# A vision block with written-out engine programs: maxima rows zeroed by a transfer, second norm from accumulators and ScalarE squares, a 64-row low part on GpSimd

## The reference

```
h = patches(images, 16x16, with 4 shifted copies) @ W + b       # 196 tokens of 192 per image
h = [cls_tok, h]                                                # 197 tokens
h = h + attention(layernorm(h))     # 6 heads of 32, scale 32**-0.5, a key-independent bias from
                                    # q . anchor; softmax over 197 keys; output product with Wo
x = clip(round(layernorm(h) / 0.02), -128, 127) as int8
h = h + (x @ weight_int8) * 0.0002 + bias
```

## Time and profile before

| what | value |
|---|---|
| median of the runs shown | 1684.41 us |
| the profiled execution, its own time | 1684.14 us |
| its span in the trace | 1682.2 us |
| TensorE busy | 1603.4 us, 95% |
| VectorE busy | 1491.4 us, 89% |
| ScalarE busy | 870.8 us, 52% |
| GpSimd busy | 822.2 us, 49% |
| first stage | to about 415 us |
| attention stage, all engines at work | about 445 to 1655 us |

### The profile page before, as it was taken

The page is one execution under the profiler, slowest core; times in us unless marked ns, Lnnn a source line. Parts: engine busy times, 40 slices in busy tenths (PEclk is TensorE's granted clock), DMA queues, the critical chain, the costliest instruction groups (busy, mean ns, idle before and its releaser), DMA issues.

```text
span 1682.2 us, 53448 instructions
## 1 busy us (share of the span) xinstructions
PE 1603.4 (95%) x16880; PEld 1426.5 (85%) x16880; DVE 1491.4 (89%) x3656; ACT 870.8 (52%) x2014; POOL 822.2 (49%) x1787
## 2 busy tenths in 40 slices
PE   3999999998499999999999999999999999999995
PEld 3999999998488888888888888888888888888884
DVE  7888888887479999999999999999999999999995
ACT  2000000000367767677767676777767776777663
POOL 3353535355025555555554555555555555555555
PEclk9999999999599999999999999999999999999997
DMA  9998999993435444444444444444444444444431
GB/s 300 271 313 292 305 299 309 292 332 131 138 130 164 152 160 137 161 150 154 144 154 159 147 151 149 161 144 157 142 159 148 159 139 156 156 153 146 153 110 37
DMA packets 213037, 303.64 MB, mean 181 GB/s; under 512 B 44656, under 2 KB 201891, under 8 KB 202868
## 3 DMA queue, kind: packets, MB, share of 16 engines
q1 hardware_dynamic: 201618, 227.16, 41.7%
q10 hardware_dynamic: 7378, 39.47, 8.1%
q0 software_dynamic: 3984, 36.28, 5.6%
HBM read 126.54 MB, written 58.29 MB: 110 GB/s over the span
## 4 chain that ended last, share of the span: by engine, by line
PE 71%; DVE 1%; POOL 1%; issue 1%; ACT 1%; ACTq 0%; DMA 0%; SPq 0%; POOLq 0%; DVEq 0%
PE o_bank L945 12%; PE bank L937 11%; PE bank L891 11%; PE s_pair L925 9%; PE bank L912 7%; PE bank L900 7%; PE bank L872 5%; PE o_bank L975 5%; PE bank L1037 2%; PE bank L1075 1%; PE o_bank L967 0%; ACTq L769 0%; DVE neg_max L1195 0%; ACT probs L1091 0%; DMA xn_in<-xn_scratch 0%
## 5 line engine op out<-in xcount | busy, mean ns | idle before, releaser
L1091 ACT ACTIVATE probs<-bank 99x396 f32<-99x396 f32 x768 | 380.5, 495 | 163.1 <-PE bank L937 156.5
L356 PE MATMUL bank<-e_t,xt 128*128 128x192 f32 x2352 | 387.0, 328 | 26.6 <-DVE xt L464 21.8
L356 PEld LDWEIGHTS bank<-e_t,xt 128*128 128x128 f32 x2352 | 385.5, 191 | 27.8 <-DVE xt L464 27.6
L1195 DVE TENSOR_REDUCE neg_max<-s_pair 99x4 f32<-99x788 f32 x384 | 374.2, 974 | 16.7 <-PE s_pair L925 15.8
L1352 POOL TENSOR_TENSOR hb<-h,ffn_bias 99x384 f32<-99x384 f32 x128 | 129.6, 1012 | 381.6 <-DVE h L1285 381.6
L937 PE MATMUL bank<-st 128*99 128x198 f32 x1536 | 296.5, 274 | 5.0 <-ACT probs L1091 5.0
L937 PEld LDWEIGHTS bank<-st 128*99 128x99 f32 x1536 | 194.9, 165 | 87.2 <-issue 80.0
L464 DVE STREAM_TRANSPOSE xt<-x_t 128x256 f32<-128x256 f32 x588 | 214.9, 416 | 44.4 <-PE bank L356 42.4
L945 PE MATMUL o_bank<-probs,vals 99*32 99x198 f32 (+1 forms) x3072 | 223.5, 337 | 0.0
L925 PE MATMUL s_pair<-st 128*99 128x198 f32 x1536 | 217.9, 264 | 3.1 <-DVE neg_max L1195 2.2
L1340 POOL TENSOR_SCALAR qx<-h,ln 99x192 f32<-99x192 f32 x256 | 199.0, 782 | 41.3 <-POOL ln L163 41.3
(11 more groups left out here) (140 smaller groups left out, 3612.2 us busy)
## 6 DMA issues: line engine op xcount, KB each, us to landing
st<-qk_hi SPq DMA_DIRECT2D x378, 198.0 KB, 2.3
st<-qk_lo SPq DMA_DIRECT2D x189, 198.0 KB, 2.3
x_t<-in_x_dram SPq DMA_DIRECT2D x26, 1344.0 KB, 20.8
x_t<-in_x_dram ACTq DMA_DIRECT2D x26, 1344.0 KB, 23.1
xn_in<-xn_scratch SPq DMA_DIRECT2D x128, 148.5 KB
h_in<-h_scratch SPq DMA_DIRECT2D x128, 148.5 KB
h_scratch<-h_t POOLq DMA_DIRECT2D x13, 1344.0 KB, 18.2
xn_scratch<-xn_t POOLq DMA_DIRECT2D x13, 1344.0 KB, 8.9
```

The source lines that it names most:

```text
L356: last = pe.matmul(token_bank(p)[:, 0:D], xt[:, p, c // 3, c % 3, :], e_t[:, row_kind(t), col, c // 3, c % 3, :], start=c == 0, stop=c == 5)
L1091: nc.scalar.activation(probs[:, n.two, h, :, :], wide(T_BANK, TC), ACT.Exp).then_inc(exp_done, 1)
L1195: nc.vector.tensor_reduce(out=neg_max[:, n.two, :, 2 * j:2 * j + 2].rearrange("p c h -> p h c"), in_=both, axis=AX_X, op=ALU.max, negate=T ...
```

## The change

The rows of maxima are set to zero by one more transfer for a pair of images (`clear_maxima`, from a tile of zeros; 2 x 6 x 396 values), so `stacked[pair]` counts ten; for that the running `shift` goes, and VectorE splits `neg_max` itself. The residual h1 is made by two instructions of 192 columns instead of one of 384, each of which also gives the sum of its row (`h_sum`). BN_STATS and `pair_factors` go. GpSimd makes the negated mean from the sum (2 columns), ScalarE squares h1 minus the mean in two ACTIVATEs of 192 columns, whose bias is that mean (one value a row) and which also give the sums of their squares (`h_var`), and GpSimd makes the factor from these with two small instructions. The 64-row low part goes from VectorE to GpSimd, behind `a_lo`, with a wait between them.

```diff
+            def clear_maxima(p):
+                if p.reuses(MOD):
+                    sp.wait_ge(st_done, p.count(H, (2 - MOD) * H))
+                sp.dma_start(q_st[MAX_HI:MAX_LO + 1:4, p.pair, :, :, :].rearrange("p h s n -> p h (s n)").bitcast(F32),
+                             zero_rows[:].unsqueeze(1).broadcast_to([2, H, 2 * TP])).then_inc(stacked[p.pair], 16)
...
@@ SyncE, odd step
                     sp.wait_ge(qklo_done, p.pair_count(3, 2))
                     stack(p, 1, 1, qk_lo)
+                    clear_maxima(p)
...
@@ ScalarE, step: behind high(p, ...), ahead of exps(c, 4)
+                if has_q:
+                    act.wait_ge(mean_done, q.count(1, 1))
+                    for cc in range(2):
+                        nc.scalar.activation(square[:, cc, :], h1[:, q.two, cc, :], ACT.Square,
+                                             bias=ln2[:, q.two, 0, cc:cc + 1],
+                                             accum_out=h_var[:, q.two, cc:cc + 1]).then_inc(var_done, 1)
                 if has_c:
                     exps(c, 4)
...
@@ VectorE, step
-                if has_e:
-                    dve.wait_ge(ahi_done, e.count(1, 1))
-                    nc.vector.tensor_tensor(a_mix[DB:DA, e.two, 1, :], att_t[0:DB, 1, :],
-                                            a_mix[0:DB, e.two, 1, :].bitcast(F32), ALU.subtract).then_inc(alo_done, 1)
                 if has_a:
                     dve.wait_ge(max_done, a.count(HG, HG))
-                    nc.vector.tensor_tensor(shift[:, a.slot, :, :], shift[:, a.slot, :, :], neg_max[:, a.two, :, :],
-                                            ALU.add).then_inc(shift_done, 1)
-                    dve.wait_ge(shift_done, a.count(1, 1))
                     if a.reuses(NS):
                         dve.wait_ge(mt_done, a.count(1, 1 - NS))
-                    nc.vector.tensor_copy(max_parts[:, a.two, :, 0:H], shift[:, a.slot, :, :]).then_inc(mpart_done, 1)
+                    nc.vector.tensor_copy(max_parts[:, a.two, :, 0:H], neg_max[:, a.two, :, :]).then_inc(mpart_done, 1)
...
-                    nc.vector.tensor_tensor(h1[:, e.two, :, :], h_in[:, e.two, :, :], rows(MISC[0]),
-                                            ALU.subtract).then_inc(h1_done, 1)
+                    for cc in range(2):
+                        last = nc.vector.scalar_tensor_tensor(out=h1[:, e.two, cc, :], in0=h_in[:, e.two, cc, :], scalar=1.0,
+                                                              in1=rows(MISC[0])[:, cc, :], op0=ALU.mult,
+                                                              op1=ALU.subtract, accum_out=h_sum[:, e.two, cc:cc + 1])
+                    last.then_inc(h1_done, 1)
...
-                if has_e:
-                    dve.wait_ge(h1_done, e.count(1, 1))
-                    for cc in range(2):
-                        last = nc.vector.bn_stats(st2[:, e.two, cc, :], h1[:, e.two, cc, :])
-                    last.then_inc(st2_done, 1)
...
@@ GpSimd, step
-                    pool.wait_ge(st2_done, q.count(1, 1))
-                    pair_factors(nc, link, st2[:, q.two, :, :], v, ln2[:, q.two, :, :].rearrange("p j c -> p c j"),
-                                 minus_half[0:TC, 0:2])
+                    pool.wait_ge(var_done, q.count(2, 2))
+                    pool.sem_inc(passed, 1)
+                    link(nc.gpsimd.tensor_scalar(var, h_var[:, q.two, :], 4.0 / D, 4.0 * LN_EPS, ALU.mult, ALU.add))
+                    link(nc.gpsimd.tensor_tensor(factor, var, minus_half[0:TC, 0:2], ALU.pow))
...
                     nc.gpsimd.tensor_tensor(a_lo[:, e.two, :], att_t[:, 0, :], a_mix[:, e.two, 0, :].bitcast(F32),
                                             ALU.subtract).then_inc(pool_lo, 1)
+                    pool.wait_ge(pool_lo, e.count(1, 1))
+                    nc.gpsimd.tensor_tensor(a_mix[DB:DA, e.two, 1, :], att_t[0:DB, 1, :],
+                                            a_mix[0:DB, e.two, 1, :].bitcast(F32), ALU.subtract).then_inc(alo_done, 1)
+                    pool.wait_ge(alo_done, e.count(1, 1))
...
                     pool.wait_ge(h1_done, e.count(1, 1))
+                    nc.gpsimd.tensor_scalar(ln2[:, e.two, 0, :], h_sum[:, e.two, :], -1.0 / D, 0.0, ALU.mult,
+                                            ALU.add).then_inc(mean_done, 1)
```

More of the change, by code:

```diff
@@ L682, in build_attention @@
     query_row = tile("query_row", [DA, 1])
-    shift = tile("shift", [TC, MOD, 2, H])
+    zero_rows = tile("zero_rows", [2, 2 * TP])
     log_sum = tile("log_sum", [DA, 2, TP])
@@ L693, in build_attention @@
     hb = tile("hb", [TC, NS, 2, D])
-    st2 = tile("st2", [TC, NS, 2, 6])
-    ln2 = tile("ln2", [TC, NS, 9, 2])
+    h_sum = tile("h_sum", [TC, NS, 2])
+    h_var = tile("h_var", [TC, NS, 2])
+    square = tile("square", [TC, 2, D])
+    ln2 = tile("ln2", [TC, NS, 3, 2])
     qx = tile("qx", [TC, NS, 2, D])
@@ L1271, in step @@
                     dve.wait_ge(mpart_done, a.count(2, 1))
[L1272 removed]
+                    nc.vector.tensor_tensor(max_parts[:, a.two, :, H:2 * H], neg_max[:, a.two, :, :],
                                             max_parts[:, a.two, :, 0:H].bitcast(F32),
@@ L1338, in step @@
                         pool.sem_inc(passed, 1)
+                    pool.wait_ge(mean_done, q.count(1, 1))
+                    pool.sem_inc(passed, 1)
                     for cc in range(2):
-                        nc.gpsimd.tensor_scalar(qx[:, q.two, cc, :], h1[:, q.two, cc, :], v[7][:, cc:cc + 1],
-                                                v[6][:, cc:cc + 1], ALU.add, ALU.mult).then_inc(ln2_step, 1)
+                        nc.gpsimd.tensor_scalar(qx[:, q.two, cc, :], h1[:, q.two, cc, :], mean[:, cc:cc + 1],
+                                                factor[:, cc:cc + 1], ALU.add, ALU.mult).then_inc(ln2_step, 1)
                 if e.within(B):
```

47 lines of the change are left out of this document (19 added, 28 removed).

## The result

The changed kernel takes 1713.01 us (median of 4 runs, 1710.79 to 1713.92), the kernel before 1684.41 us (median of 4, 1684.06 to 1688.57): 28.6 us more, ratio 1.0166 with a 95% interval of 1.0153 to 1.018. The forecast was 1709 us, with a range of its own from 1690 to 1727. The execution in the profile took 1713.92 us with a span of 1712.2; that of before took 1684.14, so 29.8 us lie between the two traces.

The account below looks back on a forecast made before the run. TensorE was taken to set the time, with only its waits to gain or lose. 35.3 - 8.7 - 1.2 = +25.4 us on 1684.14 us gave 1709.5, stated as 1709 us; own range 1690 to 1727, 8-in-10 range 1676 to 1738.

Parts of the forecast that it names:

- What bounds the kernel: Whole kernel: TensorE, busy 95% of the span, sets the time; only its waits can be given back.
- VectorE's part: Attention stage: less VectorE work removes TensorE's waits for the maxima before the first scores, -8.7 us.
- ScalarE's part: Squares ahead of exps(c, 4) make TensorE wait at score_t(c, 5): 0.57 us for two steps, 62 pairs, +35.3 us.
- S: ScalarE time the two squares take together ahead of exps(c, 4): forecast 0.81 us, between 0.51 and 1.12.
- The rooms of 0.57 and 0.48 us: Time the squares may take ahead of exps(c, 4) before TensorE waits: 0.57 us in even steps, 0.48 in odd.
- The ends: Drain: shorter norm chain from h1 to qx, 2.6 us instead of 3.8, -1.2 us; fill taken as nothing.
- GpSimd's part: Shorter norm chain keeps qx in time; the added low part has 0.22 us to spare before TensorE's load: nothing.
- the fourth: Rival: GpSimd's second low part is late and TensorE waits before L912; 1680 to 1724 us, chance 0.07.
- SyncE's part: Odd steps: one more transfer issue, about 0.68 us, fits where the queue is empty: nothing.
- The first: Rival: cheap squares, S below 0.57, so only VectorE's relief counts; 1674 to 1677 us, chance 0.22.
- The second: Rival: cost and relief cancel, S 0.57 to 0.65; within 5 us of before, 1684 us, chance 0.13.
- The third, no overlap: Rival: squares don't overlap and have the extras on top, S near 1.0 to 1.12; 1733 to 1748 us, chance 0.13.

Follow-up runs that it names:

- the floor: The step times of e8, the level against which the squares' cost is measured: a pair (one odd and one even step) takes 18.659 us.
- e7: Changed kernel with the second norm of before (BN_STATS, no squares), keeping the zeroed maxima rows and GpSimd's low part: 1683.38 us, ratio 0.9992.
- e4: Kernel before with only the 64-row low part moved from VectorE to GpSimd, behind a_lo: 1684.42 us, ratio 0.9996.
- e1: Changed kernel with both squares moved behind the copy qx_t instead of ahead of exps(c, 4): 1731.02 us, ratio 1.0277.
- e2: Changed kernel with squares in place but without their sums (variance a constant): 1686.74 us, ratio 1.0004.
- e3: Changed kernel with squares in place but no bias from a tile (mean not taken off): 1687.87 us, ratio 1.0017.
- e8: Changed kernel with squares in place but neither bias from a tile nor sums (variance a constant, norm not computed): 1672.43 us, ratio 0.9926.
- e5: e1 with the 64-row low part back on VectorE: 1700.07 us, ratio 1.0097.
- e9: Changed kernel with one square ahead of exps(c, 4) and the other behind qx_t: 1730.86 us, ratio 1.0279.
- e11: e9 with the small instruction that scales the sums and adds epsilon moved from GpSimd to VectorE, ahead of its second maxima: 1674.93 us, ratio 0.9946.
- e6: e1 with GpSimd's two low parts ahead of qx, and VectorE's subtraction of the maxima ahead of its rounding of qx: 1688.26 us, ratio 1.0022.

## Why the prediction was right, and where it was off

**What bounds the kernel.** Right. TensorE has nothing that it can give back but its waits, and what the change made or took away in waits is all of the result but some 2 us (below, the ends).

**VectorE's part, -8.7 us.** Right in kind, a little small. The pair at the floor is 18.659 us, that of before 18.826: 0.167 x 62 = 10.4 us. e7 and e4 show that it isn't spread over the three edits as VectorE's own time is: with the low part and the zeroed rows alone a pair takes 18.778 us (e7), which is 3 us of the 10.4; the norm gives the rest. VectorE's own busy time fell by 0.68 us a step (935.4 over 106 steps to 846.6 over 104), not by 0.8: its cast of the maxima now takes 0.48 us, where it took 0.175.

**ScalarE's part, +35.3 us.** The place and the mechanism were right: an idle time of 0.24 us on average at L932 in every step (25.2 us over 104; 0.20 to 0.35 were forecast), ended by the exponential that starts 1.28 us behind `high` (the forecast said 1.2). The experiments show the cause: the wait goes when the squares leave the place (e1), and shrinks with S while they stay (e2, e3, e8). The term that was mis-sized is S, 0.81 forecast and 0.88 measured. I had put the two extras of a square together as one short ACTIVATE of 0.15 us; they are two costs of 0.09 to 0.10 each, as e2 and e3 show one at a time. The rooms of 0.57 and 0.48 us were nearly right. By them S = 0.88 would cost 0.31 + 0.40 = 0.71 a pair; it cost 0.62, and S = 0.69 cost 0.255 where they say 0.33. The waiting load is 0.30 us late in even steps, as the room says, and 0.33 in odd ones; so the odd step has some 0.07 us more room than I read. The two errors, S too low and the odd room too small, lean against each other. And that S came so near has luck in it: the rows left it anywhere from 0.51 to 1.12, and 0.81 was a choice between the ends, not a reading. The term measured is 0.622 x 62 = 38.6 us.

The rule of the Trainium skill that the prediction cites ("ScalarE: Activation LUTs", section "What ACT_TABLE_LOAD costs"), an ACTIVATE that is about 93 ns longer for each pointer operand, can now be held against rows: 445 ns with the bias from a tile (e2) and 354 without (e3 and e8), 91 ns. The trace agrees. What the sum by that rule alone (1695 us) leaves out is the read of the accumulator, the other half; at the S of 0.69 that the rule gives, with the accumulator free, e2 measured 1686.74.

**The ends, -1.2 us.** Not borne out as a sum. The step read for it is right in kind: for the last image it is 2.90 us from the end of h1 (1702.02) to `qx`, against 3.8 in the earlier trace rows, where I said 2.6:
```profile
1702.02 0.19 POOL L1350 TENSOR_SCALAR ln<-h_sum 99x2 f32<-99x2 f32 x1 [2.93 <-DVE h L1280]
...
1704.92 0.99 POOL L1334 TENSOR_SCALAR qx<-h,ln 99x192 f32<-99x192 f32 x2 [0.41 <-POOL ln L1326]
```
h1 itself takes 0.2 us more, so the last image gains 0.7 us. But the drain as a whole, from the first scores of the last step to the end of the span, takes 44.67 us before and 44.91 after. Two things take the gain back. The extras of the squares are one: in e8, without them, the drain takes 42.56 us. The second low part is the other. I had priced it at nothing, and in the drain nothing covers it; with it and the old norm the drain is 1.5 us longer than before (e4). The line is that of TensorE's last output product:
```profile
1699.19 0.45 PE L907 MATMUL bank<-wo_hi,a_mix 128*99 128x192 f32 x1 [2.73 <-POOL a_mix L1343]
```
Another 2.1 us lie ahead of all steps: the first scores of the first step start at 447.85 us before and at 449.94 after. The other traces, whose first stage is the same, have them from 445.98 to 449.64, e3 at 447.67 and e8 at 449.44, so nothing shows that these 2.1 us belong to the change. From the first step's first scores to the last's it is 27.7 us more, and 2.1 + 27.7 + 0.2 = 30.0 us is the difference of the two spans.

| term | forecast, us | measured, us |
|---|---|---|
| waits for the exponential | +35.3 | +38.6 |
| VectorE's waits taken away | -8.7 | -10.4 |
| the ends (measured: the drain) | -1.2 | +0.2 |
| ahead of the first step | none | +2.1 |
| what 62 times the mean pair counts too much | none | -0.5 |
| sum | +25.4 | +30.0 (spans) |

**GpSimd's part, 0 us.** Right for the steps of this kernel, though not for the drain: `qx` comes in time, the low part is in time, nothing waits at the output product. It was right for a reason that I had only half. I counted 0.22 us of room behind the low part and took the power's 0.70 us as fixed. In the changed kernel the power starts 1.6 us before `att_t` and isn't touched. Where it starts less than 0.72 us before, all of GpSimd's chain moves by 0.8 to 1.1 us. The rival on this, the fourth, priced the meeting with `att_t` at `qx`, where it is harmless.

**SyncE's part, 0 us.** Nothing in e7, which has it, speaks against it.

**The rivals.** The first, cheap squares, is what e8 built: 1674 to 1677 forecast for S below 0.57, 1672.43 measured at S = 0.51. Its mechanism is real; the squares aren't that cheap. The second would have been S near 0.65; e2, at 0.69, came out level with before. The third, no overlap, needed S of 1.0 or more. The fourth is absent in the steps of the changed kernel and turned up in e1, e5 and e9 instead, with more force than I gave it.

## What to carry to other kernels

Before work is put ahead of an instruction that another engine waits for, read the room there in the timeline and count every row that the new work brings: a sum output is an instruction of its own and a bias from a tile isn't free. An extra of 0.1 us in a step that has no room comes back a hundred times. When such work is moved elsewhere, look at what each small instruction behind it will meet: in these kernels it wasn't the start of a GpSimd instruction that counted but whether it ended before VectorE's `att_t` began.

## What the runs showed of the hardware

- **The accumulator outputs are rows of their own.** On ScalarE an ACTIVATION_READ_ACCUMULATOR of 190 ns that delays the next instruction by 0.09 to 0.10 us; on VectorE, in the kernel after, a DVE_READ_ACCUMULATOR of 83 ns beside which the next instruction starts at once (1693.07 for both in the drain; two 192-column sums start 0.27 to 0.28 us apart).
- **A GpSimd power that is under way when `att_t` begins is held up, though it started first.** `att_t`, a VectorE instruction on two SBUF tiles, takes 0.56 us in every case. The two-column power ends 1.13 us behind the start of `att_t`, whether it had 0.04 us left (e11, 1.81 us) or 0.34 (e1, 1.50 us), so it isn't simply paused for the 0.56. Over e1, e5, e6, e9 and e11 this holds for 515 of the 518 powers that start 0.31 to 0.72 us before `att_t`: they end 1.12 to 1.14 us behind its start, while VectorE's next instruction ends anywhere from 1.12 to 1.26, so that one doesn't decide it. The three others (in e1, e6 and e9, each near 522 us) took 0.71 us although they met `att_t`; what was different there stays open. `qx` of the kernel before, which starts 0.12 us ahead of `att_t`, takes 1.55 us, and 0.99 in the drain: 0.56 more, just the time of `att_t`. No run tries another VectorE instruction in the place of `att_t`, so that it is the two SBUF tiles that matter isn't shown here. The Trainium skill ("SBUF — State Buffer", section "Who interferes with whom") says that a VectorE instruction with two SBUF inputs contends with a GpSimd instruction that reads SBUF, and that the order of issue, not the shape, decides who blocks. The trace agrees with the first half, and not with the second, if that means that the first to issue goes on undisturbed: here the one that came first was held.
- **VectorE is held up by GpSimd too, in a place where I hadn't looked.** The timeline of the kernel after, an even step:
```profile
1002.07 0.61 POOL L1343 TENSOR_TENSOR a_mix<-att_t,a_mix 64x198 fp32r<-64x198 f32 x1
...
1002.17 0.54 DVE L1250 CAST max_parts<-neg_max 99x12 fp32r<-99x12 f32 x1
```
The 12-column CAST starts 0.10 us behind GpSimd's low part and ends with it, 0.54 us later; over the stage it takes 484 ns. In the odd steps of e9, where it starts 0.07 to 0.11 us ahead of the low part, it takes 175 ns, as in the kernel before. It cost TensorE nothing here.
